# Last cross-attention step of a Perceiver layer: five score banks in rotation, values taken two units at a time

## The reference

```python
C_q = Q @ Wq_d                       # Q: layernorm(x), 8 x 64 x 512 -> 64 latent
C_kv = K @ Wkv_d                     # K: ctx, 8 x 1601 x 512 -> 32 latent
CqWqk = (C_q @ W_qk).reshape(b, n, H, LKV)           # 16 heads, 32 wide
scores = jnp.einsum('bnhl,bkl->bhnk', CqWqk, C_kv) / jnp.sqrt(LKV)
attn = jax.nn.softmax(scores, axis=-1)
V_up = (C_kv @ Wv_u).reshape(b, nkv, H, HD)
out = jnp.einsum('bhnk,bkhd->bnhd', attn, V_up)
x = x + out.reshape(b, n, H * HD)
```

## Time and profile before

| | |
|---|---|
| median of 3 runs | 892.7 us (892.52 to 893.07) |
| profiled execution | 892.23 us |
| its span in the profile | 889.8 us |
| PE, DVE, ACT, POOL busy | 850.9, 607.7, 518.0, 459.5 us |
| last step: first scores to the barrier | 249.45 to 275.75 us |

### The profile page before, as it was taken

One profiled execution on the slowest core, in us unless ns is written; L12 is line 12 of the kernel. 1 busy time (PEld: TensorE's weight loads), 2 busy tenths in 40 slices (PEclk: granted clock), 3 DMA queues, 4 the chain that ended last, 5 costly groups with the idle time before them and its releaser, 6 DMA issues.

```text
span 889.8 us, 15531 instructions
## 1 busy us (share of the span) xinstructions
PE 850.9 (96%) x5338; PEld 647.5 (73%) x5338; DVE 607.7 (68%) x1001; ACT 518.0 (58%) x1005; POOL 459.5 (52%) x294
## 2 busy tenths in 40 slices
PE   6899999999998889999999999999999999899998
PEld 4454555454534668888888888888888887788886
DVE  4756677667636278588586785867858679677784
ACT  4754646454664367476574765657756577555552
POOL 2598798787760064544545435454354544244430
PEclk9899999999998899999999999999999999999999
DMA  9553443204305405042050330503305004446521
GB/s 360 204 206 118 157 173 128 77 9 114 98 1 198 166 5 213 25 147 91 0 212 24 131 105 0 212 24 109 126 0 212 13 1 142 143 142 212 198 87 48
DMA packets 42338, 102.96 MB, mean 116 GB/s; under 512 B 7858, under 2 KB 12978, under 8 KB 41394
## 3 DMA queue, kind: packets, MB, share of 16 engines
q1 hardware_dynamic: 42002, 102.06, 32.8%
q10 hardware_dynamic: 288, 0.26, 0.1%
HBM read 96.95 MB, written 1.05 MB: 110 GB/s over the span
## 4 chain that ended last, share of the span: by engine, by line
PE 60%; DVE 2%; POOL 1%; DMA 1%; ACT 1%; issue 0%; SPq 0%; POOLq 0%; DVEq 0%
PE psum L1461 11%; PE psum L1442 10%; PE psum L1577 9%; PE psum L1515 9%; PE psum L1473 6%; PE psum L1591 4%; PE psum L1491 3%; PE psum L1500 3%; PE psum L1496 3%; PE psum L1482 1%; PE psum L1494 1%; PE psum L1492 1%; DMA ffn_raw<-in_L_ffn_mean_w_dram 1%; POOL head_probs L1954 0%; POOL ffn_quant L1974 0%; POOL ffn_raw L1974 0%
## 5 line engine op out<-in xcount | busy, mean ns | idle before, releaser
L1954 POOL TENSOR_TENSOR head_probs<-head_probs,inverse_den 128x576 f32<-128x576 f32 x128 | 147.5, 1153 | 200.9 <-DVE inverse_den L1809 200.9
L1056 DVE TENSOR_REDUCE max_part<-psum 128x1 f32<-128x804 f32 x128 | 121.2, 990 | 50.6 <-PE psum L697 50.1
L953 ACT ACTIVATE probs<-psum 128x512 f32<-128x512 f32 (+1 forms) x208 | 106.8, 607 | 57.5 <-PE psum L719 56.7
L1691 ACT ACTIVATE head_probs<-psum,neg_max 128x576 f32<-128x576 f32 x128 | 94.8, 741 | 50.3 <-DVE neg_max L1826 49.8
L1826 DVE TENSOR_REDUCE neg_max<-psum 128x1 f32<-128x576 f32 x128 | 96.9, 757 | 21.9 <-PE psum L1461 19.2
L567 POOL TENSOR_TENSOR prob_sums<-prob_sums,probs 128x1024 f32<-128x1024 f32 (+1 forms) x42 | 100.2, 2386 | 7.2 <-ACT probs L953 2.7
L567 POOL TENSOR_TENSOR prob_sums<-probs 128x1024 f32<-128x1024 f32 x30 | 71.4, 2383 | 32.9 <-ACT probs L953 32.9
L1461 PE MATMUL psum<-k_high,query_t_high 128*128 (+1 forms) x256 | 86.1, 336 | 1.9 <-DVE query_t_low L1781 1.4
L1802 DVE TENSOR_TENSOR probs_t_low<-psum,probs_t_high 128x512 fp32r<-128x512 f32 x124 | 84.8, 684 | 1.0
L719 PE MATMUL psum<-q_t,c_t 97*128 97x512 f32 (+1 forms) x208 | 75.6, 435 | 5.4 <-ACT probs L953 4.3
L1974 POOL TENSOR_TENSOR ffn_quant<-ffn_raw 128x1536 f32<-128x1536 f32 x13 | 45.6, 3509 | 67.7 <-DVE ffn_w_low L1888 26.9
(11 more groups left out here) (236 smaller groups left out, 1922.4 us busy)
## 6 DMA issues: line engine op xcount, KB each, us to landing
ctx_t_odd<-in_ctx_dram SPq DMA_DIRECT2D x4, 3202.0 KB, 10.8
ffn_raw<-in_L_ffn_w_dram SPq DMA_DIRECT2D x42, 256.0 KB, 3.7
ffn_raw<-in_L_ffn_mean_w_dram SPq DMA_DIRECT2D x42, 256.0 KB, 4.1
w_piece<-in_L_ffn_w_dram SPq DMA_DIRECT2D x21, 512.0 KB, 6.6
w_piece<-in_L_ffn_mean_w_dram SPq DMA_DIRECT2D x21, 512.0 KB, 7.7
cache<-in_ctx_dram SPq DMA_DIRECT2D x3, 3202.0 KB, 11.6
wq_nat<-in_L_attn_wq_dram SPq DMA_DIRECT2D x32, 256.0 KB, 7.4
wo_nat<-in_L_attn_wo_dram SPq DMA_DIRECT2D x32, 256.0 KB, 3.4
```

The source lines that it names most:

```text
L953: act.activation(prob_buffer(b, t)[0:rows, half * BANK:(half + 1) * BANK], psum[0:rows, n % SCORE_BANKS, :], ACT.Exp, scale=XSCALE).then_i ...
L1056: dve.tensor_reduce(max_part[:, qt, pair:pair + 1], psum[:, bank:bank + 2, 0:PIECE_KEYS], AX.XY, ALU.max).then_inc(s_max, 1)
L1691: act.activation(probs[:, qt, :].rearrange("p (a k) -> p a k", a=2), psum[:, 2 * (qt % 2):2 * (qt % 2) + 2, 0:HALF], ACT.Exp, bias=neg_max ...
L1954: pool.tensor_tensor(probs[:, qt, :], probs[:, qt, :], rden[:, qt:qt + 1].to_broadcast([P, KEYS]), ALU.mult).then_inc(s["norm"], 1)
```

## The change

In the last step the halves from 4 on rotate over five banks, 0, 1, 2, 5 and 7, and wait for the exponential of five halves before. PE waits once for what last read banks 5 and 7. The step's order is rewritten: `mix` of batch 6 comes ahead of the values, the values are taken in three visits of two units, and the first denominator round stands apart from a visit. ACT reads each half from the bank that `score_bank` gives.

```diff
+LAST_BANKS = (0, 1, 2, 5, 7)
+def score_bank(b, t, half):
+
+    n = 2 * t + half
+    if b + 1 < BATCH or n < 4:
+        return (HALVES * b + n) % SCORE_BANKS
+    return LAST_BANKS[(n - 1) % len(LAST_BANKS)]
...
-                    wait(pe, s_exp, n - SCORE_BANKS + 1)
+                    wait(pe, s_exp, n + 1 - (len(LAST_BANKS) if b + 1 == BATCH and t >= 2 else SCORE_BANKS))
...
-                    pe.matmul(psum[0:rows_of(t), n % SCORE_BANKS, :], lhs,
+                    pe.matmul(psum[0:rows_of(t), score_bank(b, t, half), :], lhs,
...
             def last_step(b):
 
+                pe.wait_ge(s_cnat, BATCH)
+                pe.wait_ge(s_shift, 2 * BATCH)
                 scores(b, 2)
                 scores(b, 3)
-                values(b, range(0, 1))
+                mix(b - 1)
                 scores(b, 4)
-                mix(b - 1)
                 scores(b, 5)
-                values(b, range(1, 2))
-                for u in range(2, UNITS - 2):
-                    scores(b, 2 * u + 2)
-                    scores(b, 2 * u + 3)
-                    values(b, range(u, u + 1))
-                    if u == 3:
-                        pe.wait_ge(s_d, 2 * b)
-                        denominator_round(b, (0, 1), True)
+                values(b, range(0, 2))
+                for t in range(6, 10):
+                    scores(b, t)
+                values(b, range(2, 4))
+                scores(b, 10)
+                scores(b, 11)
+                pe.wait_ge(s_d, 2 * b)
+                denominator_round(b, (0, 1), True)
                 scores(b, KT - 1)
-                values(b, range(UNITS - 2, UNITS - 1))
+                values(b, range(4, 6))
                 denominator_round(b, (2, 3), False)
                 last_tail(b)
```

More of the change, by code:

```diff
@@ L953, in exponential @@
                     act.activation(prob_buffer(b, t)[0:rows, half * BANK:(half + 1) * BANK],
-                                   psum[0:rows, n % SCORE_BANKS, :], ACT.Exp, scale=XSCALE).then_inc(s_exp, 1)
+                                   psum[0:rows, score_bank(b, t, half), :], ACT.Exp, scale=XSCALE).then_inc(s_exp, 1)
             def compressed(b):
```

## The result

The changed kernel took 888.8 us (median of 22 runs) beside 893.1 for the kernel before, run in turn; the ratio is 0.9945, with a 95% interval from 0.9926 to 0.9964, thus 4.9 us less (3.2 to 6.6), or 4.3 by the medians. Three executions far above the rest (960 us of the kernel before, 1,399 and 1,400 of the changed one) are left out of the ratio; without them the medians are 893.1 and 888.6. The forecast was 890.2, with 2.5 us of gain. The profiled execution took 886.92 us with a span of 884.5, so 5.3 less than in the earlier trace rows.

The account below looks back on a forecast made before the run. Neither PE nor ACT is full: three banks make each wait for the other, and the step's end hangs on PE. Fewer visits (0.6) and waits (1.8) give 2.47 us less; 892.7 - 2.5 = 890.2 us, range 887.2 to 891.8.

Parts of the forecast that it names:

- The walk: Last step, PE and ACT followed side by side: half 3 to tail falls from 17.80 to 15.33 us, 2.47 less.
- The stalls of ACT: Last step: ACT waits for scores 0.76 and 0.6 us behind the first two visits, some 1.5 in all instead of 4.2.
- What is late next: End of the step: POOL's sixth addition ends at 266.90, 0.37 us before the tail's second half; tail to mix stays 3.37.
- 0.6 for fewer visits and 1.8 for waits: Last step, split of the 2.47 us gain: 0.6 from fewer runs and visits, 1.8 from waits (2.6 to 0.8).
- The later stages: Behind the step's barrier: they keep their lengths and move with the work, so the step's gain reaches the kernel's end.
- the likeliest case: Whole kernel: the walk, with clock stretches moving with the work, gains 1.8 to 3.2 us, 889.4 to 891.0; chance 0.58.
- rival B: Stages after the step: PE's slow clock stretches shift or vanish, 1 to 3.5 us more gained, 886.7 to 889.2; chance 0.18.
- signs of being wrong: Profile after: a visit much later, POOL's end holding mix, or changed granted clock in the step or slow-stretch length against work.
- Rival A: Last step: waits only change place, gain 0.6 to 1.7 us, about 891.5; 0.20, shared with clock stretches going the wrong way.
- Rival C: Last step: PE's clock falls inside it, 893.6 to 897.0 us; 0.04, shared with a long clock stretch elsewhere.

Follow-up runs that it names:

- e1: Changed kernel with the old order of the last step put back, five banks kept; profiled once at 886.75 us.
- e2: Kernel before with the new order of the last step, three banks kept; profiled once at 894.65 us.
- e3: Kernel before with useless matmuls filling PE's idle time between tail and mix and behind mix; 893.6 us, ratio 1.0016.
- e4: Changed kernel with useless matmuls filling PE's idle time between tail and mix and behind mix; 890.6 us, ratio 0.9965.
- e6: Kernel before with useless matmuls in PE's idle time at the second barrier, ahead of the queries; 892.0 us, ratio 1.0001.
- e7: Changed kernel with useless matmuls in PE's idle time at the second barrier, ahead of the queries; 888.4 us, ratio 0.9944.
- e9: Kernel before with PE's idle time filled at both barriers; 891.8 us, ratio 0.9985.
- e10: Changed kernel with PE's idle time filled at both barriers; 890.1 us, ratio 0.9958.
- e5: Changed kernel with four useless DVE copies behind the last addition to x, delaying the next stage by 2.28; 890.8 us, ratio 0.9969.

## Why the prediction was right, point by point

**The walk** was right. It gave 15.33 us from half 3 to the tail. Measured were 15.28, and 15.28 to 15.29 in the other profiles of that step. Counted from half 3, `mix` of batch 6 came at 1.41 (forecast 1.43), the three visits at 3.59, 8.10 and 12.68 (forecast 3.59, 8.11, 12.73), the first two left after 1.86 and 1.85. The stalls of ACT were 0.65 and 0.48, forecast 0.76 and 0.6, and the total 1.1, forecast some 1.5.

**What is late next.** POOL's sixth addition followed without a gap and ended 15.74 behind half 3, forecast 15.82. It held nothing: the matmuls of the tail's second half, the first to need it, start at 266.92, 0.42 behind those before them, as in the kernel before. Tail to `mix` and to the barrier stayed.

**Where the 2.5 us come from.** I had split them into 0.6 for fewer visits and 1.8 for waits. e1 shows that the waits give 2.38 by banks alone, with all six visits kept, and e2 that the order gives nothing with three banks; with five it adds 0.14. The sum was right, this split was not. By the walk's own costs fewer runs and visits save PE some 0.6 us, but the longer runs bring waits of their own (0.67 in the run of eight, where e1's runs of four have none), and one pays the other.

**The later stages** were the term in doubt, and here the likeliest case was wrong in size. The forecast took them as moving with the work, which gave 889.4 to 891.0, and put 0.18 on more gain from the clock (rival B, 886.7 to 889.2). Measured is 888.8, a gain of 4.3 by the medians and 3.2 to 6.6 by the interval, so some 1.8 us more than the walk gave. The time lies within the stated range only because that range took in B as well; so much of it is luck. One of the prediction's own signs of being wrong was also there: the slow stretches did not keep their place against their work. In the profiled pair B happened in full: the stretch on the queries was not there (2.49) and that on the keys cost less (0.47). That B also made the 1.8 us of the medians is not shown, as below. Rival A fell with e1 and the stalls of the profile. Rival C did not happen in the profiles of the changed kernel, but in that of e2: with three banks and the new order the clock did fall inside the step. The Trainium skill, page "TensorE: Matmul & The Clock Gate", section "A second HAM failure mode: psum-queue depth-cycling", tells of a kernel in which PE, going through its banks, idled for short times so often that its clock swung to and fro. The rows of the kernel before, whose clock stayed at 1.00 in the step, did not agree with it. The profile of e2 would fit it, with three banks and PE waiting for ACT at five halves in a row, though its clock fell in the step only once, for 3.4 us.

**What stays open.** Where the 1.8 us beyond the step come from in the medians is not settled. For the clock: at both barriers the profiles show stretches that cost from 0 to 2.7 us, and with fillings there the kernels were not 4.3 apart but 2.9 (e3, e4), 3.6 (e6, e7) and 1.7 (e9, e10). Against it speak three things. e5, delayed to the old barrier time, kept 2.3 of the gain (0.4 to 5.2 by its interval). The time at the lower level does not order the medians: each timed execution has its mean granted clock, and in the four later series the kernel before had a median of 892.3 us both at 0.988 (16 executions; its profile had this value, with three stretches of 6.8 us each, the first near 40 us) and at 0.992 (31 executions), while the changed kernel had 888.7 at 0.992 (10 executions, 886.9 to 890.7). And the rest behind the first scores of the attention scatters by 2.7 us from profile to profile at a granted clock of 1.00. Beside this, 6 of the 21 executions of the kernel before in the ratio took 896 us or more, and 2 of the 20 of the changed one 895; the medians hardly see these. The medians of the kernel before in its five series lie between 892.5 and 893.3, so a difference of some tenths between two series says nothing. What is shown is that the step itself gives 2.5, with 15.20 to 15.42 us in nine profiles with five banks against 17.80 to 17.82 in four with three banks and the old order.

## What to carry to other kernels

When one engine fills banks for another and leaves for longer work in between, the number of banks must cover that absence: write both engines' queues side by side with their spacings. Here the gain of more banks came out to a tenth of a us that way. Batching visits without more banks made it worse here, and with five banks it hardly mattered. Once a step of a few us is shortened, the rest of the kernel can move by as much again (in the profiled pair 2.5 from the step, 2.8 from elsewhere), so judge the edit by the stretch that it touches, in several profiles, beside the time.

## What had not been expected of the hardware

The granted clock of PE could fall inside a stretch in which PE was recorded busy 11.69 of 13 us (e2), behind a run of eight scores of which the last five started 0.49 apart, where 0.22 is the unhindered spacing. Work put into PE's idle time did not always keep the clock up: in e10 PE was given matmuls up to 0.30 us before the next stage began at 272.81, then idled 2.08 us for DVE's normalised x, and the clock fell at about 278.1, with PE busy again since 276.85, and stayed at the lower level for 6.8 us of full work. And a slow stretch of the same length, 6.8 us, cost 0 to 1.4 us on the stage of the keys, by how far behind the wait for DVE it reached, 2.7 in e10, and 2.5 on the queries, where 12 matmuls were all there was. So at one length its place made its price.
